# The variance of eight heads summed by ScalarE's accumulator, in place of a VectorE reduction

## What is computed

```python
Y = jnp.einsum('bhst,bhtv->bhsv', scores, V)
Y = jnp.transpose(Y, (0, 2, 1, 3))
mu = Y.mean(-1, keepdims=True)
var = Y.var(-1, keepdims=True)
Yn = ((Y - mu) / jnp.sqrt(var + EPS)).reshape(b, s, h * dv) * gn_weight + gn_bias
gate = X @ W_G
gate = gate * jax.nn.sigmoid(gate)
return gate * Yn @ W_O
```

## Time and profile before

| | |
|---|---|
| time, median of 3 runs | 949.45 us (949.44 to 951.26) |
| the profiled execution's own time | 948.74 us |
| its span in the trace | 946.9 us |
| PE busy | 888.8 us, 94% of the span |
| DVE busy | 895.9 us, 95% |
| ACT busy | 528.5 us, 56% |
| POOL busy | 443.7 us, 47% |
| chain that ended last | PE 91%, DVE 5%, POOL 2%, ACT 1% |

### The profile page before, as it was taken

One profiled execution on the slowest core, in us unless ns is written; L12 is line 12 of the kernel. 1 busy time (PEld: TensorE's weight loads), 2 busy tenths in 40 slices (PEclk: granted clock), 3 DMA queues, 4 the chain that ended last, 5 costly groups with the idle time before them and its releaser, 6 DMA issues.

```text
span 946.9 us, 21085 instructions
## 1 busy us (share of the span) xinstructions
PE 888.8 (94%) x8258; PEld 798.1 (84%) x8258; DVE 895.9 (95%) x2220; ACT 528.5 (56%) x1331; POOL 443.7 (47%) x343
## 2 busy tenths in 40 slices
PE   0169999999999999999999999999999999999997
PEld 0158988898989899889988998998899889989986
DVE  5899999999999999999999999999999999999995
ACT  1345565556556655665555566556655655565553
POOL 3564544553454445444544444554445344444543
PEclk9999999999999999999999999999999999999999
DMA  9000000000000000000000000000000000000000
GB/s 281 40 1 12 24 12 24 23 24 13 24 23 19 18 24 24 12 24 24 24 12 24 24 19 17 23 24 12 24 23 24 14 24 23 18 19 24 12 7 17
DMA packets 28259, 24.95 MB, mean 26 GB/s; under 512 B 9088, under 2 KB 27648, under 8 KB 27904
## 3 DMA queue, kind: packets, MB, share of 16 engines
q1 hardware_dynamic: 20224, 18.95, 6.5%
q10 hardware_dynamic: 7936, 4.66, 1.7%
HBM read 15.21 MB, written 8.39 MB: 25 GB/s over the span
## 4 chain that ended last, share of the span: by engine, by line
PE 91%; DVE 5%; POOL 2%; ACT 1%; DMA 0%; issue 0%; SPq 0%; DVEq 0%; POOLq 0%
PE quad L775 11%; PE quad L773 11%; PE quad L774 11%; PE quad L844 4%; PE quad L908 4%; PE bank L850 3%; PE bank L855 3%; PE quad L901 3%; PE bank L774 3%; PE bank L775 3%; PE bank L773 3%; PE bank L830 3%; PE bank L862 3%; PE quad L869 3%; PE quad L878 2%; PE quad L877 2%
## 5 line engine op out<-in xcount | busy, mean ns | idle before, releaser
L392 POOL TENSOR_TENSOR h_quot<-h,h_inv 128x704 f32<-128x704 f32 x64 | 88.9, 1389 | 266.2 <-DVE h_inv L607 266.2
L388 POOL TENSOR_TENSOR rstd<-var_eps,power 128x9 f32<-128x9 f32 x67 | 158.0, 2358 | 38.6 <-DVE var_eps L557 38.5
L774 PE MATMUL quad<-w_gu_lo,xT_hi 128*128 128x352 f32 x512 | 165.1, 322 | 0.0
L775 PE MATMUL quad<-w_gu_hi,xT_lo 128*128 128x352 f32 x512 | 165.1, 322 | 0.0
L773 PE MATMUL quad<-w_gu_hi,xT_hi 128*128 128x352 f32 x512 | 165.0, 322 | 0.0
L376 POOL TENSOR_TENSOR zT_lo<-zT,zT_hi 128x256 fp32r<-128x256 f32 x64 | 51.8, 809 | 164.6 <-ACT zT_hi L677 164.6
L775 PEld LDWEIGHTS quad<-w_gu_hi,xT_lo 128*128 128x128 f32 x512 | 96.2, 188 | 0.0
L773 PEld LDWEIGHTS quad<-w_gu_hi,xT_hi 128*128 128x128 f32 x512 | 96.2, 188 | 0.0
L774 PEld LDWEIGHTS quad<-w_gu_lo,xT_hi 128*128 128x128 f32 x512 | 96.1, 188 | 0.0
L384 POOL TENSOR_TENSOR qk<-qk_cos,qk_sin 128x512 f32<-128x512 f32 x64 | 82.9, 1295 | 7.1 <-DVE qk_sin L531 6.5
L689 ACT ACTIVATE silu<-quad 128x352 f32<-128x352 f32 x64 | 29.8, 465 | 92.2 <-PE quad L775 92.2
(11 more groups left out here) (147 smaller groups left out, 2849.5 us busy)
## 6 DMA issues: line engine op xcount, KB each, us to landing
x_in<-in_L_attn_X_dram SPq DMA_DIRECT2D x64, 128.0 KB, 2.1
out_dram<-y_out SPq DMA_DIRECT2D x64, 128.0 KB, 1.7
sin<-const_sin_dram ACTq DMA_DIRECT2D x1, 2048.0 KB, 11.1
cos<-const_cos_dram ACTq DMA_DIRECT2D x1, 1024.0 KB, 6.4
raw<-in_L_ffn_w_down_dram SPq DMA_DIRECT2D x2, 352.0 KB, 4.0
raw<-in_L_ffn_w_gate_dram SPq DMA_DIRECT2D x1, 512.0 KB, 3.9
raw<-in_L_ffn_w_up_dram SPq DMA_DIRECT2D x1, 384.0 KB, 5.4
w_qkvg<-in_L_attn_W_Q_dram ACTq DMA_DIRECT2D x2, 128.0 KB, 5.0
```

The costliest lines, as they stand in the source:

```text
L388: pool.tensor_tensor(rstd[:], var_eps[:], power[:], ALU.pow).then_inc(rstd_ready, 1)
L392: pool.tensor_tensor(blocks(h_quot[:]), blocks(h[:]), spread(h_inv[:]), ALU.mult).then_inc(h_divided, 1)
L774: pe.matmul(out, hi[:, k], w_lo[:, k], start=False, stop=False)
L775: return pe.matmul(out, lo[:, k], w_hi[:, k], start=False, stop=stop)
```

## The change

On ACT the one `Square` over 256 features becomes eight, one for each head of 32 features, and each has an accumulator output: the sum of its 32 squares goes straight to that head's column of `moments`. The last of the eight raises `y_var`. DVE's reduction L548 goes, with its wait for `squared`; the semaphore `squared` goes too. `y_sq` is still written and nobody reads it any more. DVE's `h_grid` gets a wait for `h_diffed`, a semaphore that DVE itself raises some ten instructions earlier in the same step (L518). Everything else stands as it was.

```diff
                 if exists(i - 1):
                     t = i - 1
-                    dve.wait_ge(squared, t + 1)
-                    dve.tensor_reduce(moments[:, 2:], heads(y_sq[:]), AX_X, ALU.add).then_inc(y_var, 1)
-                if exists(i + 1):
...
                 if exists(i - 1):
                     t = i - 1
+                    dve.wait_ge(h_diffed, t + 1)
                     dve.scalar_tensor_tensor(h_grid[:], h_magic[:], LEAST, h_diff[:], ALU.max, ALU.subtract).then_inc(h_gridded, 1)
...
                 if exists(i - 1):
                     t = i - 1
                     act.wait_ge(y_ready, t + 1)
-                    act.activation(y_sq[:], b_y[:, 0:D], ACT.Square, scale=HD ** -0.5).then_inc(squared, 1)
+                    for head in range(H):
+                        dims = slice(head * HD, (head + 1) * HD)
+                        ins = act.activation(y_sq[:, dims], b_y[:, dims], ACT.Square, scale=HD ** -0.5, accum_out=moments[:, 2 + head:3 + head])
+                    ins.then_inc(y_var, 1)
```

More of the change, by code:

```diff
@@ L199, in block_kernel @@
         summed = sem("summed")
-        y_var = sem("y_var")
         x_diffed = sem("x_diffed")
@@ L235, in block_kernel @@
         z_high = sem("z_high")
-        squared = sem("squared")
+        y_var = sem("y_var")
         x_abs = sem("x_abs")
@@ L544, in step @@
                     dve.tensor_tensor(y_out[:, t % 2, :], b_out, x_in[:, t % SLOTS, :], ALU.add).then_inc(summed, 1)
-                if exists(i - 1):
-                    t = i - 1
-                    dve.wait_ge(squared, t + 1)
-                    dve.tensor_reduce(moments[:, 2:], heads(y_sq[:]), AX_X, ALU.add).then_inc(y_var, 1)
                 if exists(i + 1):
```

## The result

| | before | changed kernel |
|---|---|---|
| median | 950.27 us (5 runs, 949.44 to 951.26) | 954.81 us (5 runs, 953.97 to 955.49) |
| ratio to before | 1 | 1.0049, 95% interval 1.0034 to 1.0064 |
| span of the profiled execution | 946.9 us | 952.2 us |
| DVE busy | 895.9 us (95%) | 852.5 us (90%) |
| ACT busy | 528.5 us (56%) | 601.0 us (63%) |

The change makes the kernel 0.5% slower: 4.5 us, where 53 were forecast. The sign is right; the size is far off, and the time lies near rival (a), a little on the slow side of its knee. One execution in this study, of the kernel with PE's transposes swapped, took 2236 us for no reason that its record shows, and is left out of the comparisons.

The account below looks back on a forecast made before the run. PE's own work was taken to bound the kernel at 13.69 us a step; a path of 12.42 + 2.11 = 14.53 us adds 52 us over 62 steps, plus 0.8 at the end, giving 1002 us, range 950 to 1062.

Parts of the forecast that it names:

- rival (a): ACT's squares and write-outs all overlap, 1.27 us or less, and fit the cover; 949 to 952 us, chance 0.22.
- PE sets the step before, DVE's saving is worth nothing: PE's own work makes the 13.69 us step; DVE's 0.33 us a step, 21 us in all, gains nothing.
- That distance is the cover of the change: On ACT and DVE, x_diff starts 1.03 us after the Square; this was said to cover the new work.
- The accumulator is written out by a second instruction of about 171 ns: On ACT, each square's accumulator write-out priced as an extra instruction with no elements, 171 ns, an estimate.
- A sum cannot be written before its last square is in, so I expect that pair to run one after the other: On ACT, write-out waits for its own square, next square overlaps it; eight take 2.11 us to x_magic.
- the four ways in the forecast's list: ACT's eight squares and write-outs up to x_magic, by degree of overlap: 0.74, 1.27, 2.11 or 2.95 us; 2.11 taken.
- The path, 12.42 us beside the squares: From x_magic over x_diff, y_hat and PE's L855 to the next Square; with 2.11 us of squares, 14.53 us.
- Slower, 0.86: Chance given to the changed kernel being slower; faster by over 0.2% had 0.02, within 0.2% 0.12.
- `x_diff` drops to 0.42 us: On DVE, x_diff starts after POOL's sum is over and takes 0.42 instead of 0.80 us.
- PE would first wait at the scores and then a little more at `y_hat`: PE waits for DVE's h at L844 by most of a microsecond, then a little more at L855.
- Rival (c), the clock: PE's new waits lower its granted clock, 1.6 us more a step, 98 us on top, 1100 us; chance 0.05.
- The end, 0.8 us: After the last tile's Square, var_eps starts some 2.25 us later instead of 1.44, 0.8 us more.

Follow-up runs that it names:

- PE's transposes swapped: Changed kernel with PE's x transposes of the next tile put ahead of those of y_hat and gate; 950.96 us, ratio 1.0008.
- the kernel of seven pairs: Changed kernel with seven of the eight squares and their accumulator reads, the eighth head's variance not computed; 950.37 us, ratio 1.0004.
- ten pairs: Changed kernel with two more squares with accumulators, to spare tiles, ahead of the eight; 977.95 us, ratio 1.0294.
- one in ACT's together with one in DVE's: Changed kernel with x_magic ahead of the eight squares on ACT and h_grid ahead of var_eps on DVE; 950.66 us, ratio 1.0005.

## Why the prediction was right and wrong, point by point

- *PE sets the step before, DVE's saving is worth nothing*: right. Shown by the kernel of seven pairs, where DVE is busy 10 us less in 200 and the ratio is 1.0004. The "about 0.3 us to spare" of DVE is 0.41 by the earlier trace rows (5.95 us in 200).
- *"That distance is the cover of the change"* (1.03 us from the `Square` to `x_diff`): wrong, and not what the sum used. In the changed kernel `x_diff` starts 87.96 - 86.09 = 1.87 us after the first square, 0.84 later than before, and the step grows by only 0.08. The shorter `x_diff` and the slack of `y_hat` ahead of its transposes are cover too.
- *The accumulator is written out by a second instruction of about 171 ns*: right that it exists, and a little low as a duration. 512 reads of 194 to 255 ns, 223 in the mean, stand in the trace.
- *"A sum cannot be written before its last square is in, so I expect that pair to run one after the other"*: this is the step that failed, the term of the squares. The read starts 0.09 us after its square's start, with the square still running. Eight pairs take 1.38 us to `x_magic`, not 2.11, and this term alone turns 7 us into 52. Of the four ways in the forecast's list, "everything overlaps" (1.27) is the one that happened, a little slower; a dependence was argued where the trace had only rows on how instructions overlap.
- *The path, 12.42 us beside the squares*: right. Its terms as listed add up to 12.40; the hand-over stands in it with 0.12, and with 0.1 in the path over `h`. With 1.38 in it the sum is 13.80 against 13.69, 0.11 x 62 = 7 us, some 957 us for 954.8 measured. Of its terms, in the step at 86 us: `x_magic` with hand-over 0.49 for 0.45, `x_diff` to `y_hat` 5.03 for 5.03, hand-over 0.06 for 0.1, L854 to the next square 6.90 for 6.82. This one step became 0.14 us longer (13.86 for 13.72); the mean over all is 0.08.
- *Slower, 0.86*: the sign came out right, but not by the forecast's reason. With the overlap as it is, the squares end only 0.08 us a step beyond what PE's work covers, and with one head fewer nothing would have been lost. The sign is in part luck.
- *`x_diff` drops to 0.42 us*: right, a median of 426 ns. The Trainium skill ("SBUF — State Buffer", Who interferes with whom) says that a DVE instruction with two SBUF inputs contends with a GpSimd instruction that reads SBUF. The traces agree with it, in the other direction too: moved 0.33 us further into POOL's sum, `x_diff` took 1.08 us.
- *PE would first wait at the scores and then a little more at `y_hat`*: wrong for this change. At eight pairs only the path over `y_hat` is over PE's own step. The two differ by 0.11 us; at ten pairs both waits are there.
- *Rival (a)*: its mechanism is what happened, with its knee at 1.27 us (measured: between 1.21 and 1.38). Its "949 to 952" was short by some 3 us, as the squares lie 0.11 us beyond the knee; it had 0.22 of the chance. The Trainium skill ("ScalarE: Activation LUTs", What ACT_TABLE_LOAD costs) gives 186 ns + 0.833 ns an element and an overlap of about 93 ns, from which an estimate of 120 ns follows for each square. That is too high for a 32-element square, measured at 79 ns from start to start, and without the reads too low for the pair, 172 ns.
- *Rival (c), the clock*: it did not happen. Even with 1.3 us of waiting in each step the granted clock stayed at 1.00, the level of 2.4 GHz.
- *The end, 0.8 us*: 0.4 measured from the last `yT` on.

What stays open: why the durations in a long train of short ACT instructions grow (179 to 241 ns for the same square) while the starts keep their distance. No run separates that. The cost of a pair beyond its 0.172 us, some 0.015 us a step, is only in part accounted for: 0.07 us over eight pairs in the hand-over from `x_magic` to `x_diff`.

## What to carry to other kernels

Price a run of short instructions by the distance of their starts, and keep overlap as the default until a row shows a drain; an argued dependence is not a row. Then work out the whole path around one step and the length at which it meets the bound: here seven pairs were free, the eighth cost 4.5 us and each further one 11.6 us, so half a microsecond, three pairs, decided between nothing and 3%. When work moves to an engine with idle time, look at what stands right behind it there: idle time that comes only after an instruction for which another engine waits does not help. A swap in PE's stream alone, or one in ACT's together with one in DVE's, gave the loss back as far as can be measured.

## What the runs showed of the hardware

- ACT's accumulator output is a second instruction, ACTIVATION_READ_ACCUMULATOR, 223 ns in mean here, started 0.09 us after its square without waiting for it to end. A pair of 128 x 32 takes 0.172 us from start to start, a square alone 0.079.
- PE can lose 0.1 us a step with a busy time of 200.00 in 200 us and hardly a wait in the list. The distance between two weight loads showed it (0.28 us and 0.43 in the median), and in part PEld's busy time; the count of matmuls in a stretch did not.
- `x_diff`, which runs beside POOL's sum, gave back most of what was gained by starting it sooner: it took 0.43 us behind the sum, 0.80 when it started in the sum's second half, 1.05 to 1.08 when it started a third of a microsecond sooner, and DVE's busy time did not fall though it had one instruction less in each step.
